# One of a unit's 32 half turns of scores leaves VectorE for ScalarE and GpSimd, and the maxima are turned by a DMA

## The reference

```
q, k, v = (proj(wq, bq), proj(wk, bk), proj(wv, bv))
scale = 1.0 / math.sqrt(H)
scores = jnp.einsum('bhqd,bhkd->bhqk', q, k) * scale
attn = jax.nn.softmax(scores, axis=-1)
out = jnp.einsum('bhqk,bhkd->bhqd', attn, v)
...
x = _layernorm(x + _L0_attn_ref(x, ...), axis=-1)
x = _layernorm(x + _L0_ffn_ref(x, ...), axis=-1)
```

## Time and profile before

| | |
|---|---|
| runs | 443.45 us median of 3 (443.38 to 444.6) |
| profiled execution | span of 441.5 us from the first to the last instruction; the median of the runs is 1.95 us above it |
| TensorE busy | 427.8 us, 97% of the span |
| VectorE busy | 386.5 us, 88% |
| ScalarE busy | 367.7 us, 83% |
| GpSimd busy | 90.3 us, 20% |

### The profile page before, as it was taken

The page is one execution under the profiler, slowest core; times in us unless marked ns, Lnnn a source line. Parts: engine busy times, 40 slices in busy tenths (PEclk is TensorE's granted clock), DMA queues, the critical chain, the costliest instruction groups (busy, mean ns, idle before and its releaser), DMA issues.

```text
span 441.5 us, 9824 instructions
## 1 busy us (share of the span) xinstructions
PE 427.8 (97%) x3496; PEld 227.0 (51%) x3498; DVE 386.5 (88%) x719; ACT 367.7 (83%) x694; POOL 90.3 (20%) x142
## 2 busy tenths in 40 slices
PE   8999999999999999999999999999899899999995
PEld 4543544444444444444444443544333488877884
DVE  6799999999999999999999999999884577657636
ACT  4487989998998999989899899999899886678762
POOL 9730000100000010000001002373311263046103
PEclk9999999999999999999999999999999999999999
DMA  6567741111130110113011001021021000000101
GB/s 165 176 196 129 270 147 33 44 28 28 48 122 25 45 31 28 27 48 122 25 46 33 26 27 49 14 43 47 15 39 50 13 8 1 1 2 2 48 1 48
DMA packets 17117, 24.88 MB, mean 56 GB/s; under 512 B 5169, under 2 KB 9009, under 8 KB 16689
## 3 DMA queue, kind: packets, MB, share of 16 engines
q1 hardware_dynamic: 16464, 23.68, 19.3%
q10 hardware_dynamic: 608, 0.59, 0.5%
HBM read 15.08 MB, written 7.60 MB: 51 GB/s over the span
## 4 chain that ended last, share of the span: by engine, by line
PE 76%; DVE 10%; ACT 5%; SPq 3%; DMA 2%; issue 2%; POOL 0%; POOLq 0%; DVEq 0%; ACTq 0%
PE ps L1369 24%; PE ps L1291 20%; PE ps L1479 16%; DVE negmax L977 9%; PE ps L1353 8%; ACT arena L664 2%; DMA parts_q<-arena 2%; PE ps L1223 2%; PE ps L1234 1%; PE ps L1423 1%; PE ps L1319 1%; PE ps L1263 1%; SPq L463 1%; SPq L435 1%; ACT v_pad L722 1%
## 5 line engine op out<-in xcount | busy, mean ns | idle before, releaser
L977 DVE TENSOR_REDUCE negmax<-ps 128x1 f32<-128x512 f32 x458 | 275.8, 701 | 1.8 <-PE ps L1291 1.5
L664 ACT ACTIVATE arena<-ps 128x512 f32<-128x512 f32 x360 | 190.0, 606 | 19.3 <-PE ps L1353 14.1
L1353 PE MATMUL ps<-qx,kx 64*128 64x512 f32 x512 | 171.3, 451 | 0.9 <-DMA qx<-mT 0.6
L1291 PE MATMUL ps<-kx,qx 61*128 61x512 f32 x468 | 160.2, 441 | 0.6 <-DMA qx<-parts_q 0.5
L1291 PEld LDWEIGHTS ps<-kx,qx 61*128 61x128 f32 x468 | 75.1, 184 | 88.6 <-DVE negmax L977 79.3
L1369 PE MATMUL ps<-arena,v_pad 128*32 128x256 f32 (+3 forms) x1328 | 104.8, 407 | 2.8 <-ACT arena L664 2.8
L664 ACT ACTIVATE hf<-ps 128x512 f32<-128x512 f32 x152 | 83.2, 604 | 9.4 <-PE ps L1353 8.4
L1353 PEld LDWEIGHTS ps<-qx,kx 64*128 64x128 f32 x512 | 78.9, 184 | 18.6 <-ACT arena L664 11.8
L1479 PE MATMUL ps<-hid,w_high 128*128 128x512 f32 (+1 forms) x296 | 68.3, 388 | 0.8 <-issue 0.4
L1479 PEld LDWEIGHTS ps<-hid,w_high 128*128 128x128 f32 x296 | 54.2, 188 | 12.3 <-issue 0.8
L1369 PEld LDWEIGHTS ps<-arena,v_pad 128*32 128x32 f32 x1328 | 28.5, 108 | 37.1 <-issue 30.7
(11 more groups left out here) (107 smaller groups left out, 317.2 us busy)
## 6 DMA issues: line engine op xcount, KB each, us to landing
qx<-parts_q SPq DMA_DIRECT2D x60, 64.0 KB, 2.1
late_sb<-in_late SPq DMA_DIRECT2D x3, 1280.0 KB, 5.5
kx<-parts_k SPq DMA_DIRECT2D x56, 64.0 KB, 2.2
parts_q<-prt SPq DMA_DIRECT2D x3, 512.0 KB, 6.4
parts_q<-arena SPq DMA_DIRECT2D x3, 512.0 KB, 8.3
xT_sb<-in_xT SPq DMA_DIRECT2D x4, 256.0 KB, 4.2
xT_sb<-arena SPq DMA_DIRECT2D x28, 32.0 KB
prt<-den SPq DMA_DIRECT2D x7, 128.0 KB
```

Of the source, the lines that this page charges most:

```text
L664: nc.scalar.activation(probs(n // HG)[:, heads(n), :], ps[:, PLAN["score", n][0], :], ACT.Exp, scale=SCALE).then_inc(exp_done, 1)
L977: nc.vector.tensor_reduce(negmax[:, t // TURNS % 2, m % 2, h * QT + q:h * QT + q + 1], ps[:, MAX_BANK + m % 4, :], AX.X, ALU.max, negate=T ...
L1291: nc.tensor.matmul(ps[:, half_bank(m), :], qx[at, slot, qc, h, q * P:(q + 1) * P], kx[at, slot, h, part * C:(part + 1) * C], start=True, s ...
L1353: nc.tensor.matmul(ps[:, bank, :], kx[at, slot, h % PAIR, kt * P:(kt + 1) * P], qx[at, slot, qc, h % PAIR, :], start=True, stop=True)\
```

## The change

Five things change.

- **One half a unit.** In units 2 to 15, one of the 32 halves (the ninth, tenth or eleventh, the one that stands last in its group) is not reduced by VectorE. ScalarE copies it, negated, from PSUM to SBUF behind the group's exponentials (`copy_beside`), and GpSimd takes its minimum by halving: nine levels of a subtraction, a minimum with zero and an addition (`take_beside`). TensorE waits with the half that reuses the bank for ScalarE's copy, and ScalarE waits with the next copy until GpSimd has ended the one before.
- **GpSimd closes the rows.** The closing minimum of the two halves is taken by GpSimd in three steps ahead of the four splitting steps (`split_max`), not by VectorE.
- **Maxima turned by a DMA.** From unit 1 on SP issues a transposing DMA of the split maxima (`turn_max` of SP), GpSimd waits for it and widens the result from bf16 (`widen_max`), and SP then spreads it as before. TensorE's turn and ScalarE's copy remain for unit 0 alone.
- **The weights' rounding** goes from ScalarE to GpSimd, two slices in each of the units 10 to 14 and one in unit 15 (`halve_w`); GpSimd's addition of the output bias goes behind unit 15.
- The loops of SP, VectorE and GpSimd are written out, and the first banks of the round are in another order.

```
+BESIDE_FROM = 8
+W_UNIT = 10
-FIRST_BANKS, LATE_BANKS = [7, 0, 6, 1], (4, 5)
+FIRST_BANKS, LATE_BANKS = [7, 6, 0, 1], (4, 5)
...
+def copied_halves():
+
+    halves = []
+    for u in range(2, U_ALL):
+        m = 2 * TURNS * u + BESIDE_FROM
+        while (m - AHEAD) % RUN != RUN - 1:
+            m += 1
+        halves.append(m)
+    return halves
...
+            def turn_max(i, w):
+
+                sp.wait_ge(max_split, i * PER + w + 1)
+                sp.dma_start_transpose(mT_half[:, w % 2, :], mpart[:, w % 2, :]).then_inc(max_across[w % 2], 16)
...
-            with sp.Fori(0, ITERS - 1) as i:
-                load_max(i, 1)
+            for i in range(ITERS - 1):
+                turn_and_load_max(i, 1)
...
                     load_q(g, slot, 0)
+                    turn_max(i, 2 * slot + 2)
...
+            def copy_beside(n):
+
+                m = BESIDE_HALVES[n]
+                act.wait_ge(max_scores, m + 1)
+                if n > 0:
+                    act.wait_ge(beside_step, BESIDE_STEPS * n)
+                nc.scalar.activation(beside[:], ps[:, half_bank(m), :], ACT.Copy, scale=-1.0)\
+                   .then_inc(beside_out, 1)
...
+                pool.wait_ge(max_taken, taken((w + 1) * 2 * TURNS))
+                if w > 0:
+                    nc.gpsimd.tensor_tensor(mrest[:], negmax[:, w % 2, 1, :], negmax[:, w % 2, 0, :], ALU.subtract)\
+                      .then_inc(max_merged, 1)
+                    pool.wait_ge(max_merged, merged + 1)
+                    nc.gpsimd.tensor_scalar(mrest[:], mrest[:], 0.0, None, ALU.min).then_inc(max_merged, 1)
+                    pool.wait_ge(max_merged, merged + 2)
+                    nc.gpsimd.tensor_tensor(negmin[:, w % 2, :], negmax[:, w % 2, 0, :], mrest[:], ALU.add)\
+                      .then_inc(max_merged, 1)
...
+                width = C // 2
+                while width:
+                    a, b = beside[:, 0:width], beside[:, width:2 * width]
+                    out = a if width > 1 else negmax[:, u % 2, m % 2, h * QT + q:h * QT + q + 1]
+                    nc.gpsimd.tensor_tensor(a, a, b, ALU.subtract).then_inc(beside_step, 1)
+                    pool.wait_ge(beside_step, done + 1)
+                    nc.gpsimd.tensor_scalar(a, a, 0.0, None, ALU.min).then_inc(beside_step, 1)
+                    pool.wait_ge(beside_step, done + 2)
+                    nc.gpsimd.tensor_tensor(out, a, b, ALU.add).then_inc(beside_step, 1)
+                    pool.wait_ge(beside_step, done + 3)
+                    done += 3
+                    width //= 2
...
+            def widen_max(w):
+
+                pool.wait_ge(max_across[w % 2], 16 * ((w + 1) // 2))
+                if w > 1:
+                    pool.wait_ge(mrow_in[w % 2], MROW_INC * (w // 2))
+                nc.gpsimd.tensor_copy(mT[:, w % 2, :], mT_half[:, w % 2, :]).then_inc(max_copied, 1)
...
+            def halve_w(n):
+
+                if n == 0:
+                    pool.wait_ge(in_w, 16 * (ITERS - 1))
+                nc.gpsimd.tensor_copy(half(w_high[:, n, :]), w_sb[:, n, :]).then_inc(w_rounded, 1)
...
+            def turn_maxima(u):
+
+                if u >= 2:
+                    take_beside(u)
+                if u >= W_UNIT:
+                    for n in range(2 * (u - W_UNIT), min(2 * (u - W_UNIT) + 2, SLICES)):
+                        halve_w(n)
+                g = u // QC + 1
+                if u % QC == 1 and 2 <= g < G_ALL:
+                    pool.wait_ge(pv_done, (g - 1) * QC * KT)
+                    stage_v(g, g % 2)
+                split_max(u)
+                widen_max(u)
...
             def turn_half(i, m):
 
-                dve.wait_ge(max_scores, i * (2 * PER * TURNS) + m + 1)
+                m += i * (2 * PER * TURNS)
+                dve.wait_ge(max_scores, m + 1)
...
+                if m in BESIDE_HALVES:
+                    return
...
+                elif m - 4 in BESIDE_HALVES:
+                    pe.wait_ge(beside_out, BESIDE_HALVES.index(m - 4) + 1)
```

More of the change, by code:

```diff
@@ L89 @@
 GROUPS_ALL = RUNS + STEPS_ALL - (TAIL - 1)
-TURN_AT = {min((2 * TURNS * (w + 1) - 1 - AHEAD) // RUN + 3, RUNS + 1): w for w in range(1, U_ALL)}
+def copied_halves():
[6 more added lines that the diff above has]
+    return halves
 def heads(n):
@@ L139, in bank_plan @@
     for g in range(-RUN_BEFORE, GROUPS_ALL):
-        if g in TURN_AT and g < RUNS:
-            place(("max", TURN_AT[g]))
         for n in scores_of(g):
@@ L146, in bank_plan @@
             place(("score", n))
-        if g in TURN_AT and g >= RUNS:
-            place(("max", TURN_AT[g]))
         w = unit_from(g)
@@ L161, with taken @@
 PLAN = bank_plan()
+BESIDE_HALVES = copied_halves()
+def taken(m):
+    return m - sum(n < m for n in BESIDE_HALVES)
+BESIDE_STEPS = 3 * (C.bit_length() - 1)
 WO_BANK, X1T_BANK, INEXACT_BANK = [2, 3, 6, 7], [2, 3, 6, 7], 2
@@ L173 @@
 HF_STEPS = max(k for k in range(TAIL) if k % 3 == 2) + 1
-W_STEPS = range(0, 2 * SLICES, 2)
-W_RUNS = [RUNS - 26 + 5 * n // 2 for n in range(SLICES)]
 STAGES = [(name, 2 * b + c) for b in range(B) for name in ("gate", "h1", "h2") for c in range(2)]
@@ L291, in build @@
         z = sb("z", [P, 2, TILES, D])
+        beside = z[:, 0].rearrange("p t d -> p (t d)")
         any_more = sb("any_more", [1, 1])
@@ L296, in build @@
         ps = ctx.enter_context(nc.psum_tensor("ps", [P, 8, C], F32))
-        def turned(w):
-            return ps[:, PLAN["max", w][0], :].bitcast(BF16)[:, 0:P]
+        first_turned = ps[:, PLAN["max", 0][0], :].bitcast(BF16)[:, 0:P]
         in_x = [sem(f"in_x{c}") for c in range(NC_)]
@@ L340, in build @@
         max_turned = sem("max_turned")
+        max_across = [sem(f"max_across{s}") for s in range(2)]
         max_copied = sem("max_copied")
@@ L699, in _ @@
                     exp(n)
+                    if n == scores_of(g)[-1]:
+                        for m in turn_halves(g):
+                            if m in BESIDE_HALVES:
+                                copy_beside(BESIDE_HALVES.index(m))
                     if g >= RUNS and n % HG == 1:
@@ L889, in left_gate @@
                                             ALU.subtract).then_inc(gate_ready, 1)
-            for k in range(STEPS):
-                if k % KT == 3 and k // KT + 1 < PER:
-                    split_max(ITERS - 1, k // KT + 1)
-                if k in W_STEPS:
-                    left_w(W_STEPS.index(k))
-                if k == KT:
-                    pool.wait_ge(in_mid, 32)
-                    nc.gpsimd.tensor_tensor(xres[:], xres[:],
-                                            bo_bc[:, :].unsqueeze(1).broadcast_to([P, TOK // P, D]),
-                                            ALU.add).then_inc(xres_ready, 1)
+            for u in range(1, U_ALL):
+                turn_maxima(u)
+            pool.wait_ge(in_mid, 32)
+            nc.gpsimd.tensor_tensor(xres[:], xres[:], bo_bc[:, :].unsqueeze(1).broadcast_to([P, TOK // P, D]),
+                                    ALU.add).then_inc(xres_ready, 1)
             for c in (0, 1):
@@ L1000, in turn_halves_from @@
                 for m in range(m0, m1):
+                    if m % (2 * TURNS) == 0:
+                        dve.wait_ge(max_split, i * PER + m // (2 * TURNS) - 1)
                     turn_half(i, m)
-                    if m % (2 * TURNS) == 0:
-                        larger(i, m // (2 * TURNS) - 1)
-            with dve.Fori(0, ITERS - 1) as i:
+            for i in range(ITERS - 1):
                 turn_halves_from(i, 2 * WHOLE, 2 * WHOLE + 2 * PER * TURNS)
@@ L1333, in bank_free, with turn_first_max @@
                 else:
-                    pe.wait_ge(max_taken, n)
-            def turn_max(w):
-                pe.wait_ge(max_split, w + 1)
-                bank_free(PLAN["max", w][1])
-                nc.tensor.transpose(turned(w), mpart[:, w % 2, :], ident_bf[:])\
-                  .then_inc(max_turned, 1)
+                    pe.wait_ge(max_taken, taken(n))
+            def turn_first_max():
+                pe.wait_ge(max_split, 1)
+                nc.tensor.transpose(first_turned, mpart[:, 0, :], ident_bf[:]).then_inc(max_turned, 1)
             def score(n):
@@ L1450, in _ @@
             for g in range(-RUN_BEFORE, GROUPS_ALL):
-                if g in TURN_AT and g < RUNS:
-                    turn_max(TURN_AT[g])
                 halves, ns = turn_halves(g), scores_of(g)
```

81 lines of the change are left out of this document (31 added, 50 removed).

## The result

The changed kernel takes **449.43 us** (median of 6 runs, 447.1 to 450.62), the kernel before on the same chip 443.73 (442.95 to 444.6): 1.0138 times as long, 95% interval 1.012 to 1.0155. I had forecast 441.

A forecast was written before the change was run, and what follows sets the result against it. VectorE was taken to set the pace, TensorE close behind. Terms -9.5 + 3.1 + 3.7 - 0.3 + 0.4 = -2.6 took the span from 441.5 to 438.9, a time of 441 us; range 437 to 449.

The forecast's parts named there:

- VectorE, -9.5 + 0.4: Units 2 to 15: one reduction and closing minimum less each on VectorE, 9.5 us saved, with 0.4 allowed for friction.
- the third rival: TensorE takes over: one more hold for ScalarE every unit makes TensorE need 18.7 a unit; 442.5 us, no change, chance 0.20.
- T = 2.7: Time of the transposing DMA of maxima, from SP's issue until GpSimd goes on: 2.7 us.
- the plain-fast rival: The transposing DMA is as fast as a plain transfer, 2.3 us, giving 438.5 us; chance 0.18.
- The floor under T: Least time for the transposing DMA: nothing on SP lands faster than a small plain transfer, 2.1 us.
- Unit 1, +3.1: At unit 1 the transposing DMA and GpSimd's widening lie bare before SP's spread, adding 3.1 us.
- GpSimd, +3.7: GpSimd runs late from unit 10 on; its 3.7 us lateness at unit 15's split is bare, earlier waits inside it.
- The end, -0.3: After the last reduction: minimum, split and normalisation take 2.9 in place of 3.2 us, saving 0.3.
- GpSimd becomes the bound: Slower rival: transposing DMA of 4.0 us, or 1.6 us more GpSimd work a unit, gives 448.5 us; chance 0.30.
- 0.5 more work a unit: Extra GpSimd work, in us a unit, above which the rival with GpSimd as the bound decides.

The follow-up runs named there:

- both: Changed kernel with unit 1's maxima turned ahead of SyncE's weight loads and one weight slice a unit on GpSimd from unit 4: 439.6 us, 0.9918.
- all_reduced: The kernel of both, but with no copied half or tree, VectorE reducing all 32 halves: the copied halves are worth 0.0048, some 2.1 us.
- two_left_out: The kernel of both, but the copied half and half 25 of each unit are made by TensorE and neither copied nor reduced: period 18.71 us.
- turn_ahead: Changed kernel with unit 1's maxima turned ahead of the weight loads in SyncE's queue, not behind the wait for query stores: 445.02 us, 1.0047.
- invert_later: Changed kernel with VectorE's reciprocal of the first denominators placed 10 reductions later in its order: 448.68 us, 1.013.
- gather_first: Changed kernel with SyncE gathering and moving the first 8 units' denominators and rows ahead of turning unit 13's maxima: 450.98 us, 1.0165.

## Why the prediction was wrong

The forecast of 441.0 was 8.4 us short. By its steps:

- **VectorE, -9.5 + 0.4.** The closing minimum was priced right: without it the period is 19.13, not 19.22. The reduction was not. "A unit becomes 31 x 0.598 = 18.54. TensorE's 18.1, now without turns, stays below that" is the step that failed: with the reduction gone, a unit takes 18.94. The copied halves are worth 0.0048 (both against all_reduced), 2.1 us, not 14 x 0.598 = 8.4. TensorE's 1.70 a group is right for most groups; what the step put at nothing is the hold for ScalarE. I called it occasional, and in the trace of before it already comes in every unit (157.81 - 155.54 = 2.27 for a group). With it a unit is 18.6 to 18.7, and two_left_out gives 18.71: the third rival's own condition and estimate. On that comes the copy's 0.16 to 0.20 a unit, where I had allowed 0.4 for the whole program.
- **T = 2.7.** Measured 2.4, with the median of issue to landing 2.3: the plain-fast rival was right in this. The Trainium skill (Advanced Engine Details and Errata, X-Bar Transpose (TRN2)) states that transposing DMAs are as fast as regular ones. The trace agrees: 2.3 beside 2.1 for a small plain one. Issued behind the early stores (turn_ahead) it took 6.3. The floor under T was misread, without effect: 2.1 is not the least of before, where 32 KB of q rows land in 1.9 (qx<-parts_q).
- **Unit 1, +3.1.** The wait was there; undoing it gave 4.0, of which 1.8 were the fall of the clock. The prediction named that fall as a thing that would make it wrong and gave it no price. The wait was priced 0.9 too high (3.1, about 2.2 measured), and the clock's 1.8 was missing; that the term is only 0.9 too small is in part luck.
- **GpSimd, +3.7.** The pace was close. A tree was forecast at 10.1 us; the one after 55.85 took 10.9 (to 66.74), as the TENSOR_SCALARs came to 44.3/14 = 3.2 us a tree and not 2.4. In units 10 to 13 the split ended 1.7, 2.8, 4.0 and 4.4 us later behind the last reduction than in the units before (1.3, 2.5, 3.1, 4.3 forecast). What failed is the place and the price: the 3.7 was to lie bare behind unit 15's last reduction, where the split is not late at all, and spreading the weights gave 6.8 back. From unit 10 to 13 GpSimd is the slowest (its splits end at 224.4, 244.4, 264.5 and 285.2 us, 19.9 to 20.7 apart), and its lateness reaches further than the maxima: to SyncE's queue, the gather behind it, VectorE's reciprocal, and the clock. The prediction followed the lateness to the scores and to the last split and to nothing that is queued behind SyncE's wait. That the reciprocal's wait alone gives almost nothing (invert_later) shows that these losses lie over one another; GpSimd's pace is under them all, for with the weights spread all of them go.
- **The end, -0.3.** From the last reduction to the end: 441.5 - 314.9 = 126.6 before, 126.3 after. Right by itself; the 3.7 that was to come on top did not come here.

By ratios, 0.0091 + 0.0154 for the two losses less 0.0048 for the copied halves and 0.0034 for the rest of the change (all_reduced) make 0.0163, against 0.0138 measured; the two losses overlap by 0.0025. In us the terms for VectorE and the end gave 3.6 and not 9.4, 5.8 short; unit 1 was 0.9 and GpSimd 3.1 short, less 1.1 of overlap. The rival "GpSimd becomes the bound" had the sign and nearly the time (448.5), with the point "0.5 more work a unit" passed by the tree's 0.8; but it didn't contain the clock, nor TensorE at 18.7, which was the third rival's, so that its time came so near is luck. I had weighed them as alternatives, and they came together. Against the rival I had held that the slow TENSOR_SCALAR rows of 128x4 ran beside other work, and that held: in the tree that width takes 0.22, not 0.49. The tree's 0.8 comes from the wide levels (0.846 and 0.526), for which I had taken a COPY's price.

What stays open: single executions of kernels that are alike up to unit 2 lose 3.95 (invert_later) to 5.65 us (gather_first) there, the more the longer the clock stays low, and why that differs is not shown. The profiled execution of the changed kernel is one of the longer ones. So a difference of single traces under about 1.5 us is not read here.

## What to carry to other kernels

Work taken off the engine that sets the pace is worth at most its distance to the next engine's pace, measured over a whole period with all its holds, not over the groups that look undisturbed; leaving the work out altogether, for no one to do, measured that distance here in one run. A hold that a few rows show should be counted over the whole stretch before it is called occasional. Work given to a slack engine should be spread evenly over the stretch that has the slack: moving eleven weight slices from six units to eleven gave 6.8 us back. A wait that is new on a DMA queue can be paid by everything queued behind it, as by the gather here, and a standstill of TensorE can cost a fall of the clock besides: about 1.8 us on top of 2.2 at unit 1.
